# A table of experts with one entry a tile, and the loop of the expert stage written out

## The chip, the cores and the metric

One of the eight cores of a Trainium2 chip runs the kernel. The time is the core's device time in microseconds (us); smaller is better. The engines are TensorE (PE; PEld is its loading of weights), VectorE (DVE), ScalarE (ACT), GpSimd (POOL) and SyncE (SP). Each has its own queue of instructions, and semaphores tie them together. A letter q behind an engine (ACTq, PEldq, DVEq, POOLq, SPq) marks what its queue does itself: register arithmetic, waits on semaphores, branches, loads of registers, the issue of DMAs.

## What is computed

A block of cross-attention with a gate, and behind it a mixture of experts with a gate. 8192 tokens (128 sequences of 64) of width 128; 16 heads of 64; 14 experts with a hidden width of 256, one expert a token.

```python
x = x + tanh(g_xattn[0]) * attention(layernorm(x), ctx_768, ...)     # 16 heads, D = 128
# then, over the rows n of layernorm(x), and added to x with the gate tanh(g_ffn):
logits = h @ router_w                                  # (8192, 14)
assignments = argmax(logits, axis=-1)
weights = softmax(logits)[assignments]
hid = gelu(einsum('nd,edf->nef', h, w1) + b1)          # F = 256
out = einsum('nef,efd->ned', hid, w2) + b2
moe_out = out[n, assignments[n]] * weights[n]
```

Only the expert that a token chose is worked out. The rest of the document is about that part.

## The kernel before

**Attention and routing.** The attention runs over 32 groups of 256 tokens (64 pairs of 128), from 0 to about 664 us. As the groups are done, DVE finds each token's expert, and POOL scatters the token's rows (the normalised row, the row itself, the weight, the token's number) into `rows_dram`, where every expert has a region of its own. When the counts are known, the regions are cut into tiles of 128 rows, 77 of them at most (`TILES`), and a table says for every tile in which row it starts (`row_tab`) and which expert it has (`expert_tab`).

**The table.** DVE works out both columns, with one tile a partition. PE turns them into a row in PSUM (`table_T`, L1251 to L1256): the rows' column by a transpose, the experts' column by a matmul with `pack`, a 128 x 32 matrix of powers of 16, so that four experts stand in one word, four bits each. POOL builds `pack` (`pack_rows`, L608 to L614). DVE copies the two rows into SBUF (`table_1_out`, L1671, for the first 16 tiles; `table_2_out`, L1788, for the others). An engine that needs an expert's number loads words of the table into its registers (`entries`, L297; the load is L304), shifts the word and masks it (the function `expert` in `ffn_run`, and `unit_expert`), and works out an address in the weights with one more register instruction (FUSED_REGOPS or ISA in the rows).

**The first 16 tiles ("units").** They belong to tiles that are full early. Their steps are placed by hand between the last steps of the attention, from about 664 to 709 us: `unit_T` (PE, L1271), `unit_copy` (ACT, L858), `unit_w1` (SP copies the expert's w1 into one of four buffers), `unit_W1` (PE, L1282), `unit_gelu` (ACT, L870), `unit_W2` (PE, L1297), `unit_out` (DVE, L1804 and L1806), `send_out` (POOL, L620).

**The expert stage.** The other 61 tiles run from 709.3 to 826.3 us, in `ffn_run` (L309) on ACT, PE and DVE. In step t, PE transposes tile t (L1229), multiplies tile t-2 by w1 (L1236) and tile t-4 by w2 (L1245). ACT copies the transposed tile t (L845) and applies gelu to tile t-2 (L851). DVE copies the w1 of tile t's expert from `w1_sb` into one of four buffers (L1883, "the pick"), and adds bias, weight and residual for tile t-4 (L1889, L1891). POOL scatters the finished tile to its tokens with one indirect DMA (`send_out`, L616 to L621). SP loads the next rows (`load_rows`, L428) into one of 16 buffers, when the scatter of the tile that was in it has landed.

**What is a loop.** Tiles are taken in trips of 16 (`RING`). In `ffn_run` the first trip of the stage (tiles 16 to 31) is written out with constants in its waits; trips 2 and 3 are a hardware loop, in which the waits are compared with a register; the rest is written out again. On POOL trips 1 to 3 are a loop, on SP trips 2 and 3. In `ffn_run` each trip begins with a load from `expert_tab`: four words in the first, then five words that begin one word before a group of four. The names QT, KT, V, xf, zx in rows are buffers that the attention used before.

Of the kernel before, what the change touches and what calls it, by code (L numbers as in the profile page):

```python
# [33 lines left out]
P = 128  # L34
# [9 lines left out]
PACK = 4  # L44
# [3 lines left out]
def gated_block_kernel(nc, x, ctx768, g_xattn, g_ffn, g_x, b_x, g_c, b_c, Wq, Wk, Wv, Wo,  # L48
# [29 lines left out]
    with ExitStack() as stack:  # L78
# [76 lines left out]
        pack = sb("pack", [P, P // PACK])  # L155
# [5 lines left out]
        row_tab_1, expert_tab_1 = sb("row_tab_1", [1, UNITS], I32), sb("expert_tab_1", [1, UNITS // PACK], I32)  # L161
        expert_tab = sb("expert_tab", [1, P // PACK], I32)
# [72 lines left out]
        s_pack, s_link1, s_cols1, s_tab1T, s_tab1 = sem("s_pack"), sem("s_link1"), sem("s_cols1"), sem("s_tab1T"), sem("s_tab1")  # L235
# [11 lines left out]
        f_send = sem("f_send")  # L247
# [85 lines left out]
        def unit_expert(eng, words, j):  # L333
            return eng.snap((words[j // PACK] >> (4 * (j % PACK))) & (SLOTS - 1))
# [5 lines left out]
        def _(sp):  # L340
# [53 lines left out]
            def unit_w1(j):  # L394

                e = unit_expert(sp, words, j)
# [36 lines left out]
            def load_trip(v, count):  # L433
                for i in range(count):
                    if i % PACK == 0:
                        starts = entries(mybir.EngineType.SP, row_tab, (v - 1) * RING + i, PACK, E * REGION)
                    load_rows(starts[i % PACK], i, v)

            for i in range(RING):
                load_rows(first_starts[i], i, 1)  # L440
            with sp.Fori(2, TRIPS) as v:
                load_trip(v, RING)
            load_trip(TRIPS, TILES - TRIPS * RING)
# [3 lines left out]
        def _(pool):  # L447
# [160 lines left out]
            def pack_rows():  # L608

                pool.memset(pack[:, :], 0.0).then_inc(s_pack, 1)  # L610
                for n in range(PACK):
                    pool.wait_ge(s_pack, n + 1)
                    pool.affine_select(out=pack[:, :], in_=pack[:, :], compare_op=ALU.not_equal, fill=float(SLOTS ** n), base=-n,
# [35 lines left out]
            with pool.Fori(1, TRIPS) as v:  # L649
                for i in range(RING):  # L650
                    send_out(v * RING + i, i)
# [1268 lines left out]
```

## Time and profile before

| | us |
|---|---|
| median of 3 runs | 828.7 (828.1 to 828.8) |
| the profiled execution, its own time | 832.4 |
| its span, from first to last instruction | 830.7 |
| attention and routing | 0 to about 664 |
| the 16 units, beside the end of the attention | 664 to 709.3 |
| expert stage, 61 tiles | 709.3 to 826.3 (117.0) |
| last scatter and end | 826.3 to 830.7 |

How to read it: the profiled execution's own time is 1.7 us longer than its span and 3.7 us longer than the median; a change is worked out as a difference of the profiled execution and then put on the median. All times in the text are from the start of the span.

### The profile page before, as it was taken

The page shows a single profiled execution, that of the slowest core. Times are in us where ns is not written, and L with a number is a line of the kernel's source. Part 1 is how long each engine was busy: PE and PEld are TensorE (multiplying, and loading weights), DVE is VectorE, ACT ScalarE, POOL GpSimd, SP SyncE. Part 2 cuts the span into 40 slices and gives each one's busy share as a digit, 9 for nine tenths or more (in the row PEclk, how much of TensorE's full clock was granted, in tenths as well). Part 3 has the DMA queues.
Part 4 walks back from the last instruction along what each step waited for, and adds up shares of the span by engine and source line. Part 5 has one row for each costly group of instructions (what it writes and reads, how often), then busy time and mean ns, then how long its engine had stood idle before and what let it go on. Part 6 is the DMA issues. An engine that isn't in the chain of part 4 may idle for free.

```text
span 830.7 us, 34251 instructions
## 1 busy us (share of the span) xinstructions
PE 764.7 (92%) x12698; PEld 691.8 (83%) x12699; DVE 570.7 (69%) x1518; ACT 565.9 (68%) x1172; POOL 476.4 (57%) x1038
## 2 busy tenths in 40 slices
PE   6889999999999999999999999999999977768775
PEld 6678999998899989999898999998998866657765
DVE  5366777777777777777777777777778855444444
ACT  3677877777777777777777777777777553444442
POOL 2555566666666555565666566655666545355455
PEclk8999999999999999999999999999999998787887
DMA  4740011011110111111010000010000243433330
GB/s 122 242 125 21 20 34 32 30 33 34 36 31 30 30 35 36 31 36 30 30 30 30 30 30 30 30 30 30 21 22 28 87 153 109 120 98 96 107 87 21
DMA packets 52308, 45.82 MB, mean 55 GB/s; under 512 B 14726, under 2 KB 47783, under 8 KB 52250
## 3 DMA queue, kind: packets, MB, share of 16 engines
q1 hardware_dynamic: 45770, 32.23, 13.9%
q0 software_dynamic: 5536, 12.80, 4.4%
q8 instruction: 36, 0.59, 0.3%
q14 instruction: 22, 0.18, 0.1%
q10 hardware_dynamic: 944, 0.01, 0.1%
HBM read 28.15 MB, written 15.48 MB: 53 GB/s over the span
## 4 chain that ended last, share of the span: by engine, by line
PE 84%; issue 4%; ACT 2%; another core or an unknown queue 1%; DVE 1%; ACTq 0%; POOL 0%; DMA 0%; DVEq 0%; POOLq 0%
PE psJ L960 11%; PE psJ L961 10%; PE psJ L962 10%; PE psS L1019 9%; PE psO L1059 8%; PE psT L1084 8%; PE psO L1245 4%; PE psM L1093 3%; PE psM L1094 3%; PE psM L1101 3%; PE psM L1236 2%; PE psT L1236 2%; PE psM L1124 1%; PE psM L971 1%
## 5 line engine op out<-in xcount | busy, mean ns | idle before, releaser
L521 POOL TENSOR_TENSOR probs<-probs,row_inv 128x1024 f32<-128x1024 f32 x63 | 119.7, 1900 | 22.7 <-DVE row_inv L1487 14.2
L684 ACT ACTIVATE QT<-psJ 128x512 f32<-128x512 f32 x128 | 76.4, 598 | 54.0 <-PE psJ L962 47.6
L1495 DVE TENSOR_TENSOR OT_l<-psO,OT_h 128x1024 fp32r<-128x1024 f32 x60 | 73.5, 1225 | 51.3 <-ACT OT_h L723 51.3
L684 ACT ACTIVATE KT<-psJ 128x512 f32<-128x512 f32 x128 | 77.4, 604 | 40.9 <-PE psJ L962 40.2
L1482 DVE TENSOR_REDUCE row_sum<-probs 128x16 f32<-128x1024 f32 x63 | 76.8, 1219 | 38.6 <-ACT probs L736 38.6
L730 ACT ACTIVATE PTs<-psT 128x512 f32<-128x512 f32 x126 | 75.8, 602 | 29.6 <-PE psT L1084 29.6
L1446 DVE TENSOR_REDUCE row_max<-psS 128x16 f32<-128x1024 f32 x63 | 76.2, 1210 | 17.4 <-PE psS L1019 17.4
L1019 PE MATMUL psS<-KT,QT 64*64 64x64 f32 x4032 | 82.8, 224 | 4.4 <-issue 1.0
L1019 PEld LDWEIGHTS psS<-KT,QT 64*64 64x64 f32 x4032 | 70.4, 136 | 17.6 <-issue 13.7
L1084 PE MATMUL psT<-ident,probs 128*128 128x128 f32 x504 | 80.1, 281 | 2.2 <-ACT PTs L730 1.9
L736 ACT ACTIVATE probs<-probs 128x1024 f32<-128x1024 f32 x63 | 66.4, 1054 | 21.9 <-DVE probs L1453 21.9
L564 POOL DMA_INDIRECT rows_by_expert<-rows,place_i x64 | 64.5, 1007 | 24.9 <-issue 24.8
L960 PE MATMUL psJ<-CT_h,Wk_h 96*128 96x256 f32 x256 | 77.4, 302 | 1.5 <-ACT QT L684 1.4
L960 PE MATMUL psJ<-XT_h,Wq_h 128*128 128x256 f32 x256 | 77.9, 304 | 0.1
L684 ACT ACTIVATE V<-psJ 128x512 f32<-128x512 f32 x128 | 75.4, 611 | 3.6 <-PE psJ L962 3.4
L1453 DVE TENSOR_TENSOR probs<-psS,row_max 128x1024 f32<-128x1024 f32 x63 | 76.8, 1220 | 1.2
L1059 PE MATMUL psO<-PTs,V 64*64 64x64 f32 x4096 | 74.9, 220 | 1.6 <-issue 0.9
L1059 PEld LDWEIGHTS psO<-PTs,V 64*64 64x64 f32 x4096 | 66.9, 135 | 6.2 <-issue 2.1
L961 PE MATMUL psJ<-CT_l,Wk_h 96*128 96x256 f32 x256 | 71.8, 280 | 0.0
L961 PE MATMUL psJ<-XT_l,Wq_h 128*128 128x256 f32 x256 | 71.7, 280 | 0.0
L962 PE MATMUL psJ<-XT_h,Wq_l 128*128 128x256 f32 x256 | 71.5, 279 | 0.0
L962 PE MATMUL psJ<-CT_h,Wk_l 96*128 96x256 f32 x256 | 71.5, 279 | 0.0
(297 smaller groups left out, 2165.7 us busy)
## 6 DMA issues: line engine op xcount, KB each, us to landing
V<-rows_by_expert SPq DMA_DIRECT2D x42, 129.0 KB
QT<-rows_by_expert SPq DMA_DIRECT2D x35, 129.0 KB
x_in<-in_x_dram SPq DMA_DIRECT2D x32, 128.0 KB, 2.2
x_res<-in_x_dram SPq DMA_DIRECT2D x32, 128.0 KB, 2.1
c_in<-in_ctx_dram SPq DMA_DIRECT2D x32, 96.0 KB, 2.3
KT<-w_sb SPq DMA_DIRECT2D x16, 128.0 KB, 2.0
rows_by_expert<-pad_row SPq DMA_DIRECT2D x1, 1806.0 KB, 11.6
w_sb<-in_L_ffn_w_dram SPq DMA_DIRECT2D x1, 1792.0 KB, 8.7
```

The source lines that it names most:

```text
L521: pool.tensor_tensor(pr, pr, row_inv[:, p.k % 2, :].unsqueeze(2).to_broadcast([P, 16, SEQ]), ALU.mult).then_inc(s_norm, 1)
L684: act.activation(dst, psJ[n % 2][:, :], ACT.Copy).then_inc(s_jobev, 1)
L730: act.activation(PTs[:, (p.k - 1) % 2, half, :], bank[:, :], ACT.Copy).then_inc(s_ptev, 1)
L960: pe.matmul(outs, w_h, r_h, start=True, stop=False)
L961: pe.matmul(outs, w_h, r_l, start=False, stop=False)
L962: return pe.matmul(outs, w_l, r_h, start=False, stop=True)
L1019: last = pe.matmul(psS[64 * c:64 * c + 64, col:col + SEQ], QT[part, p.par(), 2 * g + c, tok], KT[part, p.par(), 2 * g + c, tok], start=Tru ...
L1059: last = pe.matmul(psO[64 * h:64 * h + 64, 512 * b + SEQ * m:512 * b + SEQ * m + SEQ], V[part, p.par(1), p.k % 2, head * DH:head * DH + DH ...
L1084: last = pe.transpose(bank[:, P * g:P * g + P], src, ident[:, :])
L1446: dve.tensor_reduce(row_max[:, :], bank[:, :].rearrange("p (n k) -> p n k", k=SEQ), AX.X, ALU.max).then_inc(s_max, 1)
L1453: dve.tensor_tensor(probs[:, p.k % 2, :, :], psS[:, :].rearrange("p (n k) -> p n k", k=SEQ), row_max[:, :].unsqueeze(2).to_broadcast([P, 1 ...
L1482: dve.tensor_reduce(row_sum[:, :], pr, AX.X, ALU.add).then_inc(s_sum, 1)
```

## The change

The table has one entry a tile, and is no longer packed: `expert_tab` grows from 32 to 128 words, `expert_tab_1` from 4 to 16. `table_T` makes two transposes in place of a transpose and a matmul; `pack`, `pack_rows` and the semaphore `s_pack` go. An engine loads the entries of 16 to 20 tiles at once and uses them as they are, with no shift and no mask. The loops of `ffn_run`, of SP and of POOL are written out, all waits of the stage are against constants, and SP loads 16 starts of rows a trip, not four at a time. In `send_out` the increment of `f_send`, on which nothing waited, goes.

```diff
-        def ffn_run(eng, engine, ffn):
-            def experts(words, i):
-                def expert(n):
-                    at = PACK + i - n
-                    return eng.snap((words[at // PACK] >> (4 * (at % PACK))) & (SLOTS - 1))
-                return expert
-            words = [None] + list(entries(engine, expert_tab, 0, RING // PACK, 2 ** 16 - 1))
+        def ffn_run(engine, ffn, behind, ahead):
+            def experts(values, i):
+                return lambda n: values[behind + i - n]
             for i in range(RING):
-                ffn(UNITS + i, 1, i, [i - n >= 0 for n in range(5)], experts(words, i))
-            with eng.Fori(2, TRIPS) as v:
-                words = entries(engine, expert_tab, (v - 1) * (RING // PACK) - 1, RING // PACK + 1, 2 ** 16 - 1)
-                for i in range(RING):
-                    ffn(v * RING + i, v, i, [True] * 5, experts(words, i))
-            words = entries(engine, expert_tab, (TRIPS - 1) * (RING // PACK) - 1, RING // PACK + 1, 2 ** 16 - 1)
-            for t in range(TRIPS * RING, TILES + 4):
-                ffn(t, t // RING, t % RING, [t - n < TILES for n in range(5)], experts(words, t - TRIPS * RING))
+                if i == 0:
+                    values = [None] * behind + list(entries(engine, expert_tab, 0, RING - ahead, SLOTS - 1))
+                ffn(UNITS + i, 1, i, [i - n >= 0 for n in range(5)], experts(values, i))
+            for t in range(2 * RING, TILES + 4):
+                if t % RING == 0:
+                    count = min(RING - ahead, TILES - t) + behind
+                    values = list(entries(engine, expert_tab, t - UNITS - behind, max(count, 1), SLOTS - 1))
+                ffn(t, t // RING, t % RING, [t - n < TILES for n in range(5)], experts(values, t % RING))
...
-            return list(entries(engine, expert_tab_1, 0, UNITS // PACK, 2 ** 16 - 1))
-        def unit_expert(eng, words, j):
-            return eng.snap((words[j // PACK] >> (4 * (j % PACK))) & (SLOTS - 1))
+            return list(entries(engine, expert_tab_1, 0, UNITS, SLOTS - 1))
...
-                e = unit_expert(act, words, j)
+                e = words[j]
...
-                pool.sem_inc(f_send, 1)
...
-            pack_rows()
...
-            with pool.Fori(1, TRIPS) as v:
-                for i in range(RING):
-                    send_out(v * RING + i, i)
-            for t in range(TRIPS * RING, TILES):
+            for t in range(UNITS, TILES):
                 send_out(t, t % RING)
...
-                pe.matmul(psM[0:1, P:P + P // PACK], cols[:, 1:2], pack[:, :], start=True, stop=True).then_inc(done, 1)
+                pe.transpose(psM[0:1, P:2 * P], cols[:, 1:2], ident[:, :]).then_inc(done, 1)
...
-                dve.tensor_copy(expert_tab[:, :], psM[0:1, P:P + P // PACK]).then_inc(s_tab, 1)
+                dve.tensor_copy(expert_tab[:, :], psM[0:1, P:2 * P]).then_inc(s_tab, 1)
...
-            ffn_run(act, mybir.EngineType.Activation, ffn)
+            ffn_run(mybir.EngineType.Activation, ffn, 2, 2)
...
-            ffn_run(pe, mybir.EngineType.PE, ffn)
+            ffn_run(mybir.EngineType.PE, ffn, 4, 4)
...
-            ffn_run(dve, mybir.EngineType.DVE, ffn)
+            ffn_run(mybir.EngineType.DVE, ffn, 4, 0)
```

In words: a trip loads 16 entries on ACT (14 in the stage's first trip, 15 in its last), 16 on PE (12 in the first), and on DVE 16 in the first trip, 20 in the next two and 17 in the last. PE and DVE begin their loads at a word whose number divides by four, ACT at word 14, 30 and 46. At t = 80 PE and DVE load one more word each.

On DVE, at the start of the expert stage. Before, the load is four words, and a word is taken apart ahead of each pick:

```order
L304 TENSOR_LOAD expert_tab [waits s_tab]
L1883 REGISTER_ALU [waits f_w1]
L1883 ISA
L1883 COPY KT<-w1_sb 128x256
L1883 REGISTER_ALU [waits f_w1]
L1883 REGISTER_ALU
L1883 ISA
L1883 COPY KT<-w1_sb 128x256
```

And now, where the load is 16 words:

```order
L302 TENSOR_LOAD expert_tab [waits s_tab]
L1853 ISA [waits f_w1]
L1853 COPY KT<-w1_sb 128x256
L1853 ISA [waits f_w1]
L1853 COPY KT<-w1_sb 128x256
L1853 ISA [waits f_w1]
L1853 COPY KT<-w1_sb 128x256
```

The one or two REGISTER_ALU instructions ahead of each ISA are gone, and the wait now stands on the ISA that works out the address.

On ACT, in the middle of the stage, the gelu of a tile (KT is the hidden layer). Before:

```order
L845 ACTIVATE xf<-psJ 128x128 [waits f_t1]
L851 REGISTER_ALU [waits f_w2,f_w1]
L851 REGISTER_ALU
L851 ISA
L851 ACTIVATE KT<-psT,b1_sb 128x128
L851 ISA
L851 ACTIVATE KT<-psT,b1_sb 128x128
```

And now:

```order
L816 ACTIVATE xf<-psJ 128x128 [waits f_t1]
L822 ISA [waits f_w2,f_w1]
L822 ACTIVATE KT<-psM,b1_sb 128x128
L822 ISA
L822 ACTIVATE KT<-psM,b1_sb 128x128
```

Two register instructions between the wait and the ACTIVATE are gone; the order of the other work is the same. The units' gelu (L870) changes in the same way.

On PE, at the turn of the loop. Before, the branch and the load of five words stand between two tiles:

```order
L1245 MATMUL psO<-w2_sb,KT 128x128
L321 REGISTER_ALU
L321 COMPARE_AND_BRANCH
L304 TENSOR_LOAD expert_tab
L1229 MATMUL psJ<-ident,QT 128x128 [waits f_load0,f_t1ev]
L1236 MATMUL psM<-zx,KT 128x128 [waits f_gelu,f_pick,f_t1ev]
```

And now:

```order
L1216 MATMUL psO<-w2_sb,KT 128x128
L302 TENSOR_LOAD expert_tab
L1200 MATMUL psJ<-ident,QT 128x128 [waits f_load0,f_t1ev]
L1207 MATMUL psM<-zx,KT 128x128 [waits f_gelu,f_pick,f_t1ev]
```

The branch is gone; the load is still there, and is longer.

## Rows read from the trace of the kernel before

**Rows 1.** The page's fourth part: the chain that ended last, by engine.

```profile
PE 84%; issue 4%; ACT 2%; another core or an unknown queue 1%; DVE 1%; ACTq 0%; POOL 0%; DMA 0%; DVEq 0%; POOLq 0%
```

**Rows 2.** Stretches: from:to, length, busy us (count) by engine, clock, DMA.

```profile
664.00:709.30 45.30, 33.19 (x300) 28.67 (x301) 24.23 (x117) 19.46 (x61) 21.35 (x27) 0.88 0.43 132
709.30:826.30 117.00, 85.72 (x550) 78.85 (x548) 55.29 (x185) 50.58 (x183) 60.03 (x61) 0.82 0.32 90
```

**Rows 3.** Chain of waits from 664 us: start, duration, what; the units.

```profile
690.10 0.04 ACTq L870
690.13 0.03 issue
...
693.34 0.04 ACTq L870
...
693.40 0.04 ACTq L870
...
701.96 0.04 DVEq L1804
```

**Rows 4.** The table's loads (L304), 650 to 700 us: shortest/median/longest ns.

```profile
L304 SPq TENSOR_LOAD <-row_tab x2: 989/1084/1179, 654.1 to 699.5; - x2
...
L304 PEldq TENSOR_LOAD <-expert_tab x1: 518/518/518, 664.4 to 664.4; - x1
```

**Rows 5.** The same, 700 to 716 us: the start of the expert stage.

```profile
L304 PEldq TENSOR_LOAD <-expert_tab x1: 351/351/351, 708.4 to 708.4; - x1
L304 DVEq TENSOR_LOAD <-expert_tab x1: 354/354/354, 710.2 to 710.2; - x1
```

**Rows 6.** The same, 730 to 737 us: the first loads of five words.

```profile
L304 PEldq TENSOR_LOAD <-expert_tab x1: 1362/1362/1362, 733.0 to 733.0; - x1
L304 ACTq TENSOR_LOAD <-expert_tab x1: 1128/1128/1128, 734.2 to 734.2; - x1
```

**Rows 7.** DVE in order of time, start of stage: start, busy, work [idle before].

```profile
710.76 1.18 DVE L1883 COPY KT<-w_sb 128x256 f32 x4 [0.24 <-issue]
```

**Rows 8.** PE in order of time: start of stage, and turn of the loop.

```profile
711.15 1.19 PE L1236 MATMUL psM<-xf,KT 128*128 128x128 f32 x4 [0.62 <-ACT zx L845]
...
765.66 0.47 PE L1229 MATMUL psJ<-ident,QT 128*128 128x128 f32 x1 [0.67 <-issue]
```

**Rows 9.** DVE in order of time: the row that ends each long wait.

```profile
723.44 0.29 DVE L1889 TENSOR_TENSOR ysum<-psO,b_sb 128x128 f32<-128x128 f32 x1 [3.97 <-remote]
...
731.00 0.29 DVE L1889 TENSOR_TENSOR ysum<-psO,b_sb 128x128 f32<-128x128 f32 x1 [4.03 <-remote]
...
738.71 0.29 DVE L1889 TENSOR_TENSOR ysum<-psO,b_sb 128x128 f32<-128x128 f32 x1 [1.55 <-PE psO L1245]
...
746.34 0.29 DVE L1889 TENSOR_TENSOR ysum<-psO,b_sb 128x128 f32<-128x128 f32 x1 [3.31 <-remote]
```

**Rows 10.** POOL in order of time: the scatters of four tiles.

```profile
724.99 1.01 POOL L620 DMA_INDIRECT out_dram<-QT  x1 [2.67 <-DVE QT L1891]
726.31 0.98 POOL L620 DMA_INDIRECT out_dram<-QT  x1 [0.30 <-issue]
...
728.88 0.98 POOL L620 DMA_INDIRECT out_dram<-QT,V  x1 [0.31 <-issue]
732.55 1.02 POOL L620 DMA_INDIRECT out_dram<-QT,V  x1 [2.69 <-DVE QT L1891]
```

**Rows 11.** One line: what POOL's queue does for L619.

```profile
L619 POOLq EVENT_SEMAPHORE  x77: 17/17/17, 672.1 to 826.6; - x77
```

**Rows 12.** Waits from 710 to 826 us: total, times, longest.

```profile
ACT KT L851 <- remote: 12.6, 4, 4.3
...
PE psO L1245 <- ACT KT L851: 9.5, 8, 2.3
```

**Rows 13.** One line: POOL building the packing matrix (L613).

```profile
L613 POOL TENSOR_SCALAR_AFFINE_SELECT pack<-pack x4: 212/212/213, 644.1 to 645.2; 128x32 f32<-128x32 f32 x4
```

More of the change, by code:

```diff
@@ L154, in gated_block_kernel @@
         row_tab = sb("row_tab", [1, P], I32)
-        pack = sb("pack", [P, P // PACK])
         ends_1, full, cum_1, move_1 = sb("ends_1", [P, E], I32), sb("full", [P, E]), sb("cum_1", [P, E]), sb("move_1", [P, E])
@@ L160, in gated_block_kernel @@
         expert_1, row_1, cols_1 = sb("expert_1", [P, 1]), sb("row_1", [P, 1]), sb("cols_1", [P, 2])
-        row_tab_1, expert_tab_1 = sb("row_tab_1", [1, UNITS], I32), sb("expert_tab_1", [1, UNITS // PACK], I32)
-        expert_tab = sb("expert_tab", [1, P // PACK], I32)
+        row_tab_1, expert_tab_1 = sb("row_tab_1", [1, UNITS], I32), sb("expert_tab_1", [1, UNITS], I32)
+        expert_tab = sb("expert_tab", [1, P], I32)
         b1_rows = sb("b1_rows", [E * FK, P])
@@ L234, in gated_block_kernel @@
         s_row_tab = sem("s_row_tab")
-        s_pack, s_link1, s_cols1, s_tab1T, s_tab1 = sem("s_pack"), sem("s_link1"), sem("s_cols1"), sem("s_tab1T"), sem("s_tab1")
+        s_link1, s_cols1, s_tab1T, s_tab1 = sem("s_link1"), sem("s_cols1"), sem("s_tab1T"), sem("s_tab1")
         s_soft = sem("s_soft")
@@ L246, in gated_block_kernel @@
         f_w2, f_sum, f_out = sem("f_w2"), sem("f_sum"), sem("f_out")
-        f_send = sem("f_send")
         NEWT = 5 + 4 * NEWTON + 1
@@ L394, in unit_w1 @@
             def unit_w1(j):
-                e = unit_expert(sp, words, j)
+                e = words[j]
                 if j >= 4:
@@ L431, in load_rows @@
                 sp.dma_start(tile_rows[i], rows_dram[bass.ds(r, P), :]).then_inc(f_load[i], 16)
[L433 to L437, printed above, removed]
-            for i in range(RING):
[L440 to L443, printed above, removed]
+            for t in range(UNITS, TILES):
+                if t % RING == 0 and t > UNITS:
+                    first_starts = entries(mybir.EngineType.SP, row_tab, t - UNITS, min(RING, TILES - t), E * REGION)
+                load_rows(first_starts[t % RING], t % RING, t // RING)
         @block.gpsimd
@@ L606, in _ @@
             run(pool, step)
[L608 to L613, printed above, removed]
-                                       pattern=[[-PACK, P // PACK]], channel_multiplier=1).then_inc(s_pack, 1)
             def send_out(t, i):
                 pool.wait_ge(f_out, t + 1)
-                pool.sem_inc(f_send, 1)
                 pool.indirect_dma_start(out_rows, bass.IndirectOffsetOnAxis(tile_rows[i][:, ROW - 1:ROW].bitcast(I32), 0),
@@ L648, in _ @@
             send_out(15, 15)
-            with pool.Fori(1, TRIPS) as v:
-                for i in range(RING):
-                    send_out(v * RING + i, i)
-            for t in range(TRIPS * RING, TILES):
+            for t in range(UNITS, TILES):
                 send_out(t, t % RING)
@@ L860, in unit_gelu @@
             def unit_gelu(j):
-                e = unit_expert(act, words, j)
+                e = words[j]
                 at = [act.snap(e * FK + k) for k in range(FK)]
@@ L1251, in table_T @@
             def table_T(cols, ready, count, done):
-                pe.wait_ge(s_pack, PACK + 1)
                 pe.wait_ge(ready, count)
                 pe.transpose(psM[0:1, 0:P], cols[:, 0:1], ident[:, :])
-                pe.matmul(psM[0:1, P:P + P // PACK], cols[:, 1:2], pack[:, :], start=True, stop=True).then_inc(done, 1)
+                pe.transpose(psM[0:1, P:2 * P], cols[:, 1:2], ident[:, :]).then_inc(done, 1)
             def b1_T():
@@ L1286, in unit_W2 @@
             def unit_W2(j):
-                e = unit_expert(pe, words, j)
+                e = words[j]
                 at = [pe.snap(e * F + k * D) for k in range(FK)]
@@ L1673, in table_1_out @@
                 dve.tensor_copy(row_tab_1[:, :], psM[0:1, 0:UNITS]).then_inc(s_tab1, 1)
-                dve.tensor_copy(expert_tab_1[:, :], psM[0:1, P:P + UNITS // PACK]).then_inc(s_tab1, 1)
+                dve.tensor_copy(expert_tab_1[:, :], psM[0:1, P:P + UNITS]).then_inc(s_tab1, 1)
             def taken_1():
@@ L1791, in table_2_out @@
                 dve.tensor_copy(row_tab[:, :], psM[0:1, 0:P]).then_inc(s_row_tab, 1)
-                dve.tensor_copy(expert_tab[:, :], psM[0:1, P:P + P // PACK]).then_inc(s_tab, 1)
+                dve.tensor_copy(expert_tab[:, :], psM[0:1, P:2 * P]).then_inc(s_tab, 1)
             def unit_out(j):
-                e = unit_expert(dve, words, j)
+                e = words[j]
                 b2_at = dve.snap(e * D)
```

## The prediction

> **What bounds the kernel now.** I read the page's chain of waits first. PE holds 84% of it [rows 1], nearly all in the attention, whose instructions the change leaves alone. What it does touch lies behind 664 us: the 16 units (45.3 us) and the expert stage (117.0 us) [rows 2]. In the stage every engine is idle for much of the time: PE is busy 85.7 of 117.0 us, POOL 60.0, DVE 55.3, ACT 50.6 [rows 2]. So no engine's load sets its pace; the order of time must show what does.
>
> On DVE it shows that the stage goes by groups of four tiles. Four tiles pass quickly, then DVE waits for up to 4 us. The rows that end these waits stand at 723.44, 731.00, 738.71 and 746.34 us [rows 9]: 7.56, 7.71 and 7.63 us apart, 7.63 on the mean, or 1.91 us a tile. 61 tiles make 61/4 x 7.63 = 116.4 us, which is the stage. POOL has the same period: a scatter at 724.99, the next of the four 1.32 us later, the fourth from 728.88 to 729.86, then a wait of 2.69 us, and the next group at 732.55, 7.56 us after the last [rows 10]. Between the end of POOL's fourth scatter (729.86) and DVE's next row (731.00) lie 1.14 us, and from there to POOL's next scatter 1.55 us. What holds the signals back until POOL's group is over, the profile does not say (it calls the releaser "remote"); that DVE goes on 1.1 us after it is what rows show. I take the cycle to be: POOL's four scatters 4.87 us, 1.14 us, DVE and the way to POOL 1.55 us.
>
> **Writing out the loops: 0 us.** The trace holds the test. Tiles 16 to 31 are already written out, with constants in their waits, and the loop's first turn comes at 733 to 735 us, where the five-word loads stand [rows 6]. The first two spacings lie before that or across it (7.56, 7.71), the third in the loop (7.63) [rows 9]. At most 0.07 us a group speaks for the form without a loop, and one of the two spacings is longer. The turn of the loop leaves PE idle for 0.67 us ahead of a transpose [rows 8]; twice that, 1.3 us, is the bound of a gain if nothing hides it. The group's wait hides it: a turn falls into the 7.71, which is 0.08 us over the mean. I take 0.
>
> **Register instructions in the units: -0.8 us.** Here the steps of a unit wait for each other, and the chain of waits goes through ACT's queue. Ahead of a gelu stand one or two pieces of 0.04 us of L870 with 0.03 us of issue behind each: one at 690.10, two at 693.34 and 693.40 [rows 3]. The whole chain from 664 to 709.3 us holds eight such pieces on ACT and three of L1804 on DVE (one at 701.96 [rows 3]). The instruction that works out the address stays, and takes over the wait. 8 x 0.066 + 3 x 0.08 = 0.77 us. Bounds: 0, if the long waits in between take it up, and -2.1, if both steps of all 16 units were in line (16 x 2 x 0.066). I take -0.8.
>
> **The units' loads: +0.3 us.** They grow from 4 to 16 words. SP does load 16 words: 989 and 1179 ns, both in the list before 700 us; PE's load of four words takes 518 ns at 664.4 [rows 4]. PE's would end 0.5 to 0.7 us later, and the unit's first W1 stands 0.5 us behind the old end (665.44 in the chain), waiting for ACT's copy. That leaves 0.2 to 0.4 us: +0.3. The bound below is 0 (the attention's matmuls behind it are ready and give it back), the one above is in the rival.
>
> **The start of the stage: +0.75 us.** The pick of tile 16 needs DVE's load. Now: four words, 354 ns from 710.2 us [rows 5], pick at 710.76 [rows 7], PE's first W1 at 711.15 [rows 8], 0.1 us after that pick ends (711.05). The load grows to 16 words; at SP's 989 to 1179 ns [rows 4] everything behind moves by 0.64 to 0.83 us. I take 0.75. PE's own load (351 ns at 708.4 [rows 5], now 12 words, so at most SP's 989) and ACT's (14 words) end before that, so their delays are inside it. The shift and the mask ahead of the pick go as well, 0.1 us at most, and are inside the rounding.
>
> **POOL's step in the cycle: -1.0 us.** `send_out` loses the increment of a semaphore, 17 ns [rows 11], which stands between DVE's signal and the scatter. A step in a queue costs its own time and the issue gap behind it, 0.03 to 0.05 us where the chain lists it [rows 3]. 0.07 us, once a group, is 15 x 0.07 = 1.0 us. Bounds: 0 (the wait only moves to the next instruction) and -1.2. In the four scatters themselves it gains nothing, since they follow at 1.29 to 1.32 us with the queue ahead of them.
>
> **The stage's other loads: 0.** At t = 32, 48 and 64 the engines load 15 to 20 words instead of five. The five words take 1128 to 1362 ns [rows 6], more than SP's 16 (989): their start, one word before a group of four, is what makes them dear, and PE's and DVE's new loads begin on such a group. 16 words would cost 0.1 to 0.4 us less than now, 20 about as much. ACT's still begin off a group of four. On all three, the present loads fall into the 7.71 us spacing and cost 0.08 us at most. I take 0; the bounds are -0.2 and, for ACT, the rival. The one-word loads of PE and DVE at t = 80 lie ahead of the last W2, for which PE waits for ACT, as it does before other W2s [rows 12].
>
> **The table: 0.** POOL no longer builds `pack`: four steps of 212 ns at 644 us [rows 13], ahead of a wait of POOL. The second transpose has 128 columns in place of 32, and DVE's two copies are longer by a tenth or two of a microsecond; PE's path gets 0 to +0.2 us. POOL's loss of 1 us of work at 644 us is no gain, since the chain runs through PE there [rows 1]. SP's 16 starts at once instead of 4 x 0.3 us delay one row load by 0.7 us, 14 tiles before it is needed.
>
> **The sum.** -0.8 + 0.3 + 0.75 - 1.0 = -0.75, so the profiled execution would take 832.4 - 0.75 = 831.7 us. That execution is 3.7 us above the median of the runs shown; put on the median, the forecast is 828.7 - 0.8 = **827.9 us**. A measurement of this kernel tells about 0.2% from no change, 1.7 us: below 827.0 is faster, above 830.4 slower.
>
> **Rivals.**
> - *The cycle does not shorten.* If the release comes by its own clock, POOL's step gives nothing: +0.3 + 0.75 - 0.8 = +0.25, 829.0 us. The wait that moves to the next instruction speaks for it; the 0.3 us gap between scatters that no work fills also does [rows 10].
> - *The whole hand-over gets shorter (faster).* If the cycle runs over ACT and PE as well, the shift and the mask ahead of gelu (0.13 us) and of W2 (0.15 to 0.19) come out of each group: 15 x 0.28 more, about -4 us, 824 us. For it: ACT waits "remote" up to 4.3 us, and W2 waits for gelu 8 times [rows 12]. Against it: DVE's long waits end in an ysum whose W2 had been done long before, and no register step of PE is between.
> - *A load is priced by the word (slower).* Five words that begin off a group of four cost 1128 to 1362 ns [rows 6], 0.23 to 0.27 a word. ACT's three loads of 15 or 16 words begin off a group too. By the word they take 4.0 us each, 2.9 more than now. ACT's cover is its wait in a group, up to 4.3 us but 3.1 on the mean (12.6/4) [rows 12], of which 1.1 are used; so 0.9 us each come through on the mean and 2.9 at worst: +2.7 to +8.6. It decides from a load of about 3 us. With the forecast's other terms: 830.6, and up to 836 us. If all loads went by the word, DVE's at the start would cost 4.0 instead of 0.35 us, +3.65, and PE's at 664.4 +3.2; SP's 16 words in 989 ns [rows 4] speak against that. The Trainium skill (Runtime: NRT & Kernel Launch, Instruction fetch mechanics) gives about 200 ns a register even for a bulk load. By that figure, as an estimate, 16 words take 3.2 us and the start of the stage alone would lose 2.8 us. SP's row [rows 4] does not agree with it, 62 to 74 ns a word, while the five words [rows 6] do.
> - *The wait of every fourth tile goes away.* If the loop or `f_send` were behind it, the stage would run at POOL's 1.29 to 1.32 us a tile [rows 10], 61 x 1.29 = 79 us, and save 38. Against it: the waits are there in the part without a loop, too, from 723 us on [rows 9].
> - *The change does nothing to the time*: the register steps hide behind longer waits everywhere, and the loads too: 828.7.
>
> **How the numbers follow.** Forecast 0.40 (827 to 829, of it 0.14 below 827.0). Cycle as it was 0.20, nothing at all 0.04. Shorter hand-over 0.15. Load by the word 0.18, of it 0.13 above 830.4 and 0.05 (a mild one) below it. The wait gone 0.03. Faster: 0.14 + 0.15 + 0.03 = 0.32. Slower: 0.13, and 0.07 from the cases near +0.3 us whose start of the stage costs more than I think, 0.20. The same: 0.48. The range reaches to the shorter hand-over (824.0) on one side and to the load by the word with 1.4 us behind 830.6 on the other, 832.0; outside lie the lost wait, a third of the loads' case and a little on either side of the second rival, 0.2 in all.
>
> **What would show it.** In the changed profile: the units' first tile 0.3 us later and the last one 0.5 us earlier; DVE's load at 710 us about 1.0 us long, and PE's first W1 0.75 us further behind it; ACT's loads at t = 32, 48, 64 at 1.0 to 1.3 us (4 us means the rival); no two-step gap ahead of L822; DVE's long waits still every fourth tile, 7.56 us apart in place of 7.63. If the spacing is 7.3 us or less, the hand-over was longer than I read; if it is 7.63, POOL's step was free. The forecast is wrong at its root if the groups of four change their size or go away, since then the cover on which each 0 above rests is gone.

## The result

The changed kernel takes 817.98 us (median of 4 runs, 815.99 to 821.41), the kernel before beside it 828.4 (825.89 to 828.8). The ratio is 0.9886, with a 95% interval of 0.9864 to 0.9909. Two later comparisons gave 0.9832 (0.9778 to 0.9887) and 0.9867 (0.9837 to 0.9896). The change makes the kernel 1.1 to 1.7% faster, 9 to 14 us, where the forecast was 0.8 us and the range ended at 824.

The profiled execution of the changed kernel has a time of 821.4 us and a span of 819.6. Two stretches, as in [rows 2] (from:to, length, busy us and count of PE, PEld, DVE, ACT, POOL, then clock, share of the DMA engines, GB/s):

```profile
665.60:709.10 43.50, 32.01 (x273) 27.84 (x272) 23.69 (x112) 19.38 (x61) 20.89 (x26) 0.88 0.49 147
709.10:814.70 105.60, 77.66 (x549) 70.22 (x549) 53.77 (x184) 49.23 (x183) 60.49 (x61) 0.92 0.33 94
```

The matmuls, copies and scatters are the same in both kernels, but TensorE's granted clock is not: it was 0.82 in the stage before [rows 2] and is 0.92 here, and with it PE's busy time fell by 8 us. Whether that is a cause of the gain or goes with it is taken up with the put-back kernels below. The units (from the first `unit_T` to the first transpose of the stage) take 43.5 us, where they took 44.6; the expert stage 105.6 us, where it took 117.0. The rest of the difference in span is 1.5 us less in the attention, which the change leaves alone, against 2.4 us more in the first hundred and 0.5 us more behind the stage; the first hundred differ from run to run (POOL's first scatter stands between 102.3 and 107.5 us in the traces of this study). So almost all of the gain is in the expert stage, and that is the length that the experiments are compared by.

DVE's rows that answer to [rows 9] (start, busy, work, idle before and its releaser):

```profile
723.03 0.29 DVE L1859 TENSOR_TENSOR ysum<-psO,b_sb 128x128 f32<-128x128 f32 x1 [3.43 <-remote]
...
728.97 0.29 DVE L1859 TENSOR_TENSOR ysum<-psO,b_sb 128x128 f32<-128x128 f32 x1 [1.98 <-PE psO L1216]
...
730.51 0.29 DVE L1859 TENSOR_TENSOR ysum<-psO,b_sb 128x128 f32<-128x128 f32 x1 [0.66 <-PE psO L1216]
...
732.03 0.29 DVE L1859 TENSOR_TENSOR ysum<-psO,b_sb 128x128 f32<-128x128 f32 x1 [0.49 <-remote]
...
733.55 0.29 DVE L1859 TENSOR_TENSOR ysum<-psO,b_sb 128x128 f32<-128x128 f32 x1 [0.47 <-PE psO L1216]
```

The first group of four is still there. The next does not come 7.6 us later, but after 5.9, and then tile follows tile at 1.52 to 1.54 us, with no long wait. POOL shows the same, against [rows 10]: a scatter follows the last by 1.29 us within a group, and by 1.5 us where the tiles come singly:

```profile
727.18 0.98 POOL L595 DMA_INDIRECT out_dram<-QT  x1 [0.31 <-issue]
728.47 0.98 POOL L595 DMA_INDIRECT out_dram<-QT,V  x1 [0.30 <-issue]
730.44 0.98 POOL L595 DMA_INDIRECT out_dram<-QT,V  x1 [0.99 <-issue]
731.98 0.98 POOL L595 DMA_INDIRECT out_dram<-QT,V  x1 [0.56 <-issue]
733.50 0.98 POOL L595 DMA_INDIRECT out_dram<-QT,V  x1 [0.54 <-issue]
```

Counted over the whole stage: pauses of more than 2.3 us from one scatter's start to the next split the 61 scatters into 15 runs in both traces of the kernel before, most often runs of four (11 and 7 of the 15), and into 8, 6 and 11 runs in the three traces of the changed kernel, with runs of up to 14, 31 and 9.

The table's loads, as in [rows 4 to 6] (shortest/median/longest in ns, first and last start):

```profile
L302 PEldq TENSOR_LOAD <-expert_tab x6: 308/1146/1290, 665.3 to 811.3; - x6
L302 DVEq TENSOR_LOAD <-expert_tab x6: 310/1360/1445, 669.6 to 813.9; - x6
L302 ACTq TENSOR_LOAD <-expert_tab x5: 1246/3387/3566, 654.7 to 785.7; - x5
```

16 to 20 words that begin on a group of four cost PE and DVE 1.1 to 1.4 us (the shortest, 0.31, are the one-word loads at t = 80). 15 or 16 words that begin off a group cost ACT 3.4 to 3.6 us, 0.22 to 0.23 a word. The third rival priced this load rightly, and it still did not make the kernel slower.

The hand-over to a gelu in the units, in the chain of waits, against [rows 3] (start, duration, what):

```profile
684.99 0.02 issue
685.01 0.05 ACTq L841
685.06 0.05 issue
685.11 0.06 ACT KT L841
```

One instruction is left between PE's signal and the ACTIVATE: 0.12 us, where two register instructions of 0.04 us and their gaps stood ahead of it.

### The profile page after: what moved, and what is told of

Same layout as the page of the kernel before. It is cut to its first block, busy times and chain, and to the rows that moved or that the text cites. A ratio compares the mean times of both kernels' runs of the same rounds, so it can differ in the third digit from the quotient of the medians.

```text
span 819.6 us, 33480 instructions
## 1 busy us (share of the span) xinstructions
PE 757.8 (92%) x12696; PEld 684.7 (84%) x12696; DVE 569.3 (69%) x1517; ACT 564.9 (69%) x1171; POOL 477.0 (58%) x1033
## 4 chain that ended last, share of the span: by engine, by line
PE 84%; issue 4%; ACT 2%; another core or an unknown queue 1%; DVE 1%; POOL 1%; DMA 0%; DVEq 0%; ACTq 0%; POOLq 0%
PE psJ L931 11%; PE psJ L932 10%; PE psJ L933 10%; PE psS L990 9%; PE psO L1030 8%; PE psT L1055 8%; PE psM L1064 3%; PE psM L1065 3%; PE psM L1072 3%; PE psO L1216 3%; PE psT L1207 2%; PE psM L1207 2%; PE psM L1095 1%; PE psM L942 1%
```

## The experiments

The length of the stage is that from the start of its first transpose on PE to the end of its last `ysum` (the sum of W2's product and the bias) on DVE. Three traces of the changed kernel have 105.6, 107.3 and 110.4 us, two of the kernel before 117.0 and 115.7. A single trace is thus good to some 2.5 us, and small differences are read from the ratios. A ratio's interval is not the whole of its uncertainty either: the changed kernel's own three ratios lie 0.5% (4.5 us) apart. The expectations name theories by letters: A, the shorter hand-overs are the gain; B, the written-out loops are; C, ACT's long loads break up the groups; D, POOL's step ahead of the scatter does.

### Which part of the change: the table alone

`ffn_run` loads 16 to 20 entries as in the changed kernel, within the loops of before; the loops of SP and POOL and the increment of `f_send` are as before.

```diff
-            for t in range(2 * RING, TILES + 4):
+            with eng.Fori(2, TRIPS) as v:
+                values = list(entries(engine, expert_tab, v * RING - UNITS - behind, RING - ahead + behind, SLOTS - 1))
+                for i in range(RING):
+                    ffn(v * RING + i, v, i, [True] * 5, experts(values, i))
+            for t in range(TRIPS * RING, TILES + 4):
```

> The register table alone (one entry a tile, no shift and mask), with all loops and POOL's semaphore increment as before. Theory A (the shorter hand-overs between ACT, PE and DVE break up the groups of four): most of the gain, 7 to 11 us below before, about 819 us. Theory B (the loops written out bring it): within 2 us of before, 827 to 830. Theory C (the long loads of ACT, 3.4 us in the changed kernel's trace, shift the engines against each other and break the groups): as A, since these loads are in this kernel too.

Measured: 0.9888 of before (0.9819 to 0.9957); stage 110.7 us.

### The loops alone

The packed table with its shifts and masks; every loop of the stage written out.

```diff
-            with eng.Fori(2, TRIPS) as v:
-                words = entries(engine, expert_tab, (v - 1) * (RING // PACK) - 1, RING // PACK + 1, 2 ** 16 - 1)
-                for i in range(RING):
-                    ffn(v * RING + i, v, i, [True] * 5, experts(words, i))
+            for t in range(2 * RING, TRIPS * RING):
+                if t % RING == 0:
+                    words = entries(engine, expert_tab, (t // RING - 1) * (RING // PACK) - 1, RING // PACK + 1, 2 ** 16 - 1)
+                ffn(t, t // RING, t % RING, [True] * 5, experts(words, t % RING))
...
-            with sp.Fori(2, TRIPS) as v:
+            for v in range(2, TRIPS):
...
-            with pool.Fori(1, TRIPS) as v:
-                for i in range(RING):
-                    send_out(v * RING + i, i)
-            for t in range(TRIPS * RING, TILES):
+            for t in range(UNITS, TILES):
```

> The packed table with its shifts and masks, all loops on ACT, PE, DVE, SP and POOL written out with constant waits. Theory A and C: no gain, 827 to 830 us, with a spacing of 7.6 us between groups of four. Theory B: 818 to 820 us.

Measured: 0.9967 (0.9941 to 0.9993); stage 113.4 us.

### POOL's part alone

The kernel before, with POOL's loop written out and `f_send` gone.

```diff
-                pool.sem_inc(f_send, 1)
...
-            with pool.Fori(1, TRIPS) as v:
+            for t in range(UNITS, TILES):
```

> The kernel before with POOL's part of the change alone: its loop written out, and the semaphore increment ahead of each scatter gone. Theory A and C: 0 to 1.2 us below before (the term of the prediction). Theory D (POOL's step ahead of the scatter decides whether its scatters stay in groups): 4 to 10 us below before.

Measured: 0.9969 (0.9941 to 0.9996); stage 113.9 us. The windows of the three, in the order of the text:

```profile
704.20:814.90 110.70, 81.42 (x550) 73.32 (x549) 53.51 (x186) 49.12 (x183) 59.48 (x60) 0.89 0.34 98
```

```profile
705.20:818.60 113.40, 80.68 (x549) 73.74 (x549) 53.20 (x184) 50.30 (x183) 60.51 (x61) 0.89 0.33 93
```

```profile
705.00:818.90 113.90, 80.82 (x550) 73.51 (x549) 56.16 (x186) 50.59 (x183) 60.02 (x61) 0.90 0.33 94
```

The table brings about 1.1% (0.4 to 1.8) of the 1.1 to 1.7; POOL's part and the loops 0.3% each, and since the loops' kernel contains POOL's loop written out, these two may be the same 0.3%. Theory B falls. Theory D asked for 4 to 10 us; POOL's part as a whole brought 2.6 (0.3 to 4.9). What the increment of `f_send` is worth by itself isn't shown: the loops' kernel still has it and gains as much as the kernel without it.

### The register instructions, put back one engine at a time

The changed kernel, with two masks that change no value ahead of the address in the expert stage, on ACT (gelu), PE (W2) and DVE (pick) or on one of them. The trace shows them where the shift and the mask stood, with the wait on the first: 122 register instructions on each engine, where the kernel before had 106 at each of these places (every fourth tile needs a mask alone). The 21 that it had ahead of DVE's `ysum` are not put back.

```diff
+        def ops(eng, e):
+            return eng.snap(((e & 31) & 15))
...
-                    e = expert(2)
+                    e = ops(act, expert(2))
...
-                    e = expert(4)
+                    e = ops(pe, expert(4))
...
-                    at = dve.snap(expert(0) * F)
+                    at = dve.snap(ops(dve, expert(0)) * F)
```

> The changed kernel with two register instructions put back (two masks that change nothing) ahead of every gelu's address on ACT, every W2's on PE and every pick's on DVE in the expert stage. Theory A (the register instructions in the hand-overs are what the table saves): the stage goes back to 111 to 115 us, the time to 0.993 to 1.0 of before. Theory F (they don't matter in the stage; what helps is where and how long the loads are, and the rest is chance): stage 105 to 109, time 0.983 to 0.990.

> The same, on ACT alone. If the path of a tile runs over the gelu (A): half or more of what all three bring, 0.988 to 0.995. If DVE's or PE's matter: as the changed kernel, 0.983 to 0.988.

> The same, on PE alone, ahead of W2. A: 0.987 to 0.993, less than or like ACT's. If PE's queue stands idle there anyway: as the changed kernel, 0.983 to 0.988.

> The changed kernel with the two register instructions put back on DVE alone, ahead of the pick. If the path of a tile runs PE, ACT, PE, DVE and not over the pick: as the changed kernel, 0.983 to 0.988, stage 105 to 108 us. If the pick is on the path: 0.988 to 0.993, stage 109 to 113.

> The two register instructions ahead of the pick on DVE alone, a second time. If the pick is on the path of a tile: 0.3 to 0.6% above after_third. If not: within 0.2% of it.

Measured: all three 0.9975 (0.9958 to 0.9992); ACT alone 0.9924 (0.9901 to 0.9946); PE alone 0.9899 (0.9879 to 0.9919); DVE alone 0.9915 (0.9887 to 0.9943) and, a second time, 0.9887 (0.9852 to 0.9921). The stages of all, ACT and PE:

```profile
709.30:824.70 115.40, 80.70 (x549) 73.59 (x549) 52.92 (x184) 50.11 (x183) 62.46 (x62) 0.87 0.31 87
```

```profile
709.60:821.90 112.30, 82.41 (x549) 74.97 (x549) 52.72 (x184) 50.59 (x183) 60.10 (x60) 0.87 0.31 89
```

```profile
706.10:817.00 110.90, 80.17 (x550) 71.63 (x549) 54.28 (x184) 49.38 (x183) 60.86 (x61) 0.90 0.32 90
```

With all three, the stage is as long as that of before (115.7 and 117.0), and nearly the whole gain is gone, though the table, its loads and the written-out loops are those of the changed kernel. Its waits from 709 to 824.7 us are nearly those of before again (total, times, longest):

```profile
POOL out_dram L599 <- DVE QT L1865: 35.8, 17, 5.5
DVE ysum L1863 <- remote: 29.4, 10, 4.0
```

The same two in the kernel before, from 710 to 826 us:

```profile
POOL out_dram L620 <- DVE QT L1891: 40.5, 18, 5.1
DVE ysum L1889 <- remote: 28.5, 8, 4.0
```

And in the changed kernel, from 709 to 815 us:

```profile
POOL out_dram L595 <- DVE QT L1861: 24.0, 12, 5.4
DVE ysum L1859 <- remote: 15.9, 8, 4.9
```

With all three put back, the scatters stand in 15 runs again, 9 of them of four.

So theory A stands: what the table saves is the two register instructions in the hand-overs. Against 0.9862, the mean of the three comparisons of the changed kernel, ACT's are worth 0.6% (5 us, or 0.08 us a tile), PE's 0.4%, DVE's 0.2 to 0.5%, all three 1.1%. The sum of all three is clear: its interval (0.9958 to 0.9992) lies above those of all three comparisons of the changed kernel. How it divides among the engines is less so, since the changed kernel did not run beside ACT's and PE's kernels: against its highest ratio, 0.9886, ACT's are worth 0.4% and PE's 0.1%. That all three cost more than each alone (0.9975 against 0.9924, 0.9899 and 0.9915) says that they don't wholly hide each other. DVE's is the least certain: side by side with the changed kernel (0.9867 there) its second run is 0.2% above it, with intervals that overlap, and its traces have stages of 108.1 and 107.9 us, in the middle of the changed kernel's.

The rival is PE's clock, which was 0.82 and 0.84 in the two traces of before and 0.92, 0.89 and 0.86 in those of the changed kernel. It does not order the stages. With all three put back the clock is 0.87 and PE is busy for 80.7 us, and the stage takes 115.4; the third trace of the changed kernel has 0.86 and 82.7 us of busy PE, and its stage takes 110.4. The loops' and POOL's kernels have 0.89 and 0.90, and stages of 113.4 and 113.9. So the clock by itself doesn't explain the difference; whether it adds to it is not shown.

### ACT's long loads

The changed kernel, with ACT's loads begun on a group of four.

```diff
-            ffn_run(mybir.EngineType.Activation, ffn, 2, 2)
+            ffn_run(mybir.EngineType.Activation, ffn, 4, 2)
```

> The changed kernel, with ACT's table loads starting at a multiple of four words (12, 28, 44) and 18 entries long. Each load should fall from 3.4 us to 1.0 to 1.4 us. Theory A: as fast as the changed kernel or up to 6 us faster (three loads, 2 us each), 812 to 818. Theory C: the gain is lost, 825 to 830.

Measured: 0.9856 (0.9813 to 0.9898), stage 109.2 us.

```profile
L302 ACTq TENSOR_LOAD <-expert_tab x5: 1232/1364/1485, 649.3 to 781.2; - x5
```

The start of the load off a group of four is what made it dear: 18 words on a group take less than half of 16 off it. Theory C falls, since the gain stays. And the 2 us saved three times don't show in the time either. In the changed kernel ACT's idle time ahead of the copy after such a load is 3.05 us:

```profile
732.71 0.63 ACT L822 ACTIVATE KT<-psT,b_sb 128x128 f32<-128x128 f32 x2 [0.54 <-PE psT L1207]
736.38 0.28 ACT L816 ACTIVATE xf<-psJ 128x128 f32<-128x128 f32 x1 [3.05 <-issue]
```

POOL meanwhile works off the tiles that DVE had finished; that for this reason less or nothing of the wait reaches the end is my reading, and no run shows it.

### What holds PE's signals

In the first stretch of the stage, PE and ACT of the changed kernel:

```profile
719.28 0.27 PE L1200 MATMUL psJ<-ident,V 128*128 128x128 f32 x1
719.39 0.61 PE L1207 MATMUL psT<-zx,KT 128*128 128x128 f32 x4
719.84 0.61 PE L1216 MATMUL psO<-w_sb,KT 128*128 x4
```

```profile
720.80 0.63 ACT L822 ACTIVATE KT<-psM,b_sb 128x128 f32<-128x128 f32 x2 [1.30 <-issue]
722.89 0.28 ACT L816 ACTIVATE xf<-psJ 128x128 f32<-128x128 f32 x1 [1.47 <-remote]
```

By its record the transpose ended at 719.55 us, and ACT was free from 721.43, but its copy began at 722.89, 3.3 us after the transpose. DVE's ysum at 723.03, for a product whose record ends before 719.5, came at the same time. POOL was at four indirect DMAs from 717.11 to 722.06 us, the last two of them begun after the transpose had ended. Three kernels ask which part of the scatter does it. In their expectations theory P says that POOL's work on an indirect DMA holds PE's signals, theory L that the transfers do. The first replaces the indirect scatter by a plain DMA from POOL's queue to fixed rows:

```diff
-                pool.indirect_dma_start(out_rows, bass.IndirectOffsetOnAxis(tile_rows[i][:, ROW - 1:ROW].bitcast(I32), 0),
-                                        tile_out[i], None, bounds_check=TOK - 1, oob_is_err=False).then_inc(f_scat[i], 16)
+                pool.dma_start(out_rows[P * (t % 64):P * (t % 64) + P, :], tile_out[i]).then_inc(f_scat[i], 16)
```

> The changed kernel, with POOL's indirect scatter of a finished tile replaced by a plain DMA from POOL's queue to fixed rows of the output (so the tokens' order is left out; the bytes and all waits stay). Theory P (PE's completion signals are held while POOL works on an indirect DMA): the waits of 2.3 us and more on DVE go away, PE's pace of 1.0 us a tile sets the stage, and it falls from 106 us to 62 to 80. Theory L (the transfers themselves, the row loads of SP above all, hold them): the stage stays at 100 us or more.

Measured: 0.9426 (0.9376 to 0.9475); the stage takes 74.4 us.

```profile
699.40:773.80 74.40, 66.43 (x549) 63.70 (x549) 51.59 (x184) 48.44 (x183) 32.50 (x61) 0.98 0.52 150
```

```profile
727.79 0.29 DVE L1858 TENSOR_TENSOR ysum<-psO,b_sb 128x128 f32<-128x128 f32 x1
...
728.79 0.29 DVE L1858 TENSOR_TENSOR ysum<-psO,b_sb 128x128 f32<-128x128 f32 x1
...
729.79 0.29 DVE L1858 TENSOR_TENSOR ysum<-psO,b_sb 128x128 f32<-128x128 f32 x1
```

A tile a microsecond, PE's own pace, and the groups are gone; no wait of DVE for W2 is over 2.3 us. More than one thing changes here: POOL is busy for 0.54 us a scatter in place of 0.98, the rows go to other places, and PE's clock is 0.98 in place of 0.92, with 11 us less of busy time on PE. The second kernel keeps the indirect scatter and takes nearly all bytes out of SP's row loads:

```diff
-                sp.dma_start(tile_rows[i], rows_dram[bass.ds(r, P), :]).then_inc(f_load[i], 16)
+                sp.dma_start(tile_rows[i][:, ROW - 2:ROW], rows_dram[bass.ds(r, P), ROW - 2:ROW]).then_inc(f_load[i], 16)
```

> The changed kernel, where SP's row loads of tiles 32 to 76 bring only the last two of 258 columns (with the token's number; the rest of the rows stays that of an older tile, so most of the rows' data is left out). The number of transfers, waits and scatters stays, the bytes loaded fall to under 1%. Theory P: the stage stays near 106 us, with the long waits. Theory L: the stage falls below 90 us.

Measured: 0.9849 (0.9794 to 0.9905), stage 102.9 us, with 35 GB/s in place of some 95:

```profile
703.00:805.90 102.90, 79.36 (x549) 71.72 (x549) 54.76 (x186) 49.24 (x183) 59.94 (x61) 0.90 0.15 35
```

The loads' bytes are worth little or nothing; theory L falls as far as the loads go. The third kernel scatters only the first 64 rows of each of the 61 tiles:

```diff
+                n = P if t < UNITS else P // 2
-                pool.indirect_dma_start(out_rows, bass.IndirectOffsetOnAxis(tile_rows[i][:, ROW - 1:ROW].bitcast(I32), 0),
-                                        tile_out[i], None, bounds_check=TOK - 1, oob_is_err=False).then_inc(f_scat[i], 16)
+                pool.indirect_dma_start(out_rows, bass.IndirectOffsetOnAxis(tile_rows[i][0:n, ROW - 1:ROW].bitcast(I32), 0),
+                                        tile_out[i][0:n, :], None, bounds_check=TOK - 1, oob_is_err=False).then_inc(f_scat[i], 16)
```

> The changed kernel, with only the first 64 rows of each of the 61 tiles scattered (half of their output is left out). If the hold lasts as long as POOL works on an indirect DMA, and that follows the number of rows: each takes 0.5 to 0.6 us in place of 0.98, and the stage falls to 75 to 92 us. If POOL's time stays at 0.98 us and the stage at 104 to 108, the rows moved don't matter; if POOL's time halves and the stage stays, the hold isn't POOL's time.

Measured: 0.9893 (0.9866 to 0.992), stage 111.4 us. The time of an indirect DMA on POOL hardly falls with the rows, 906 ns for 64 against 983 for 128:

```profile
L596 POOL DMA_INDIRECT out_dram<-QT,V x42: 900/906/1029, 688.8 to 816.1; - x42
```

So half of the rows bring nothing, and this run could not tell POOL's time and the rows apart as it was meant to: none of my three cases came as written, since POOL's time hardly fell with the rows halved. What is shown: with plain DMAs in place of the indirect ones the stage is 31 us shorter than in the changed kernel's first trace, and neither the bytes loaded nor the number of rows scattered accounts for it. That POOL's work on an indirect DMA is what holds PE's signals fits all three runs but is not shown, and by which path it would do so stays open.

### Scatters kept apart

A memset of a tile that nobody reads behind each scatter, so that POOL's scatters can't follow at 1.29 us; then the same with ACT's loads on a group of four.

```diff
+                if t >= UNITS:
+                    pool.wait_ge(s_pace, t - UNITS)
+                    pool.memset(pace[:, :], 0.0).then_inc(s_pace, 1)
```

> The changed kernel, with a memset of 128x256 on a tile that nobody reads behind each scatter of the expert stage, on POOL, some 0.3 us each. In the changed kernel's trace the stage runs at 1.5 us a tile wherever scatters stand 1.5 us apart, and falls into groups wherever they follow at 1.29. Theory P with a window: with scatters kept apart PE's signals get through between them, few waits over 2.3 us are left, and the stage takes 93 to 100 us, 5 to 12 less than now. If only the sum of POOL's busy time counts: 61 x 0.3 = 18 us longer at most, 106 to 124 us.

> The changed kernel with the memset behind each scatter (the paced run) and ACT's loads on a group of four words. In the paced run's trace POOL goes at 1.51 us a tile, 61 x 1.51 = 92 us, and the stage takes 103.7, with 11 us lost about the three loads of ACT (3.4 us each). If these loads cost what they look like: 3 x 2 = 6 us less than paced, stage 96 to 99 us, 0.974 to 0.978 of before. If PE's and DVE's loads (1.1 to 1.4 us) cost as much: no more than 2 us less.

> The memset of 0.34 us behind each scatter, a second time. If keeping the scatters apart helps: 0.2 to 0.6% below after_third, stage 102 to 105 us. If it only trades the hold for POOL's time: within 0.2% of it.

Measured: 0.9824 (0.9784 to 0.9864) and, the second time, 0.9842 (0.9812 to 0.9872); with the aligned loads 0.9854 (0.9828 to 0.988). The stages are 103.7, 102.8 and 105.4 us.

```profile
703.60:807.30 103.70, 78.78 (x549) 70.67 (x549) 56.21 (x186) 49.72 (x183) 80.59 (x119) 0.91 0.36 103
```

I had expected 93 to 100 us if the scatters' spacing matters and 106 to 124 if only POOL's busy time counts; the first run fell between the two. POOL works 20 us more and the stage of the two paced kernels is 2 to 8 us shorter than the changed kernel's three, which speaks for the theory that PE's signals get through between scatters. Only 2 and 3 of DVE's waits ahead of a `ysum` are over 2.3 us, where the changed kernel has 5, 7 and 8. In the time it is not clear: beside the paced kernels the changed one had 0.9832 and 0.9867, so the difference is 0.1 and 0.25%, and the intervals overlap. The aligned loads bring nothing here either; I had expected 6 us, having read ACT's idle time of 3 us as the cause of the pauses in the paced run.

The changed kernel itself, twice more:

> The changed kernel once more, beside the others on the same chip: a second trace of it. 0.983 to 0.991 of before; stage 103 to 110 us.

> The changed kernel beside the next two on one chip: 0.982 to 0.990 of before, stage 105 to 108 us.

Their stages are 107.3 us, as expected, and 110.4, longer than the 105 to 108 expected. And the kernel before, whose second trace has a stage of 115.7 us:

> The kernel before, a second trace. The four other traces with shift and mask (or their like) in the stage have stages of 113.4, 113.9 and 115.4 us; so 113 to 117 us here, with most waits of DVE in groups of four.

## Why the prediction was wrong

**What bounds the kernel: right in the place, wrong in the path.** The gain is in the units and the stage, and no engine's load sets the pace. But the cycle that I took for the stage (POOL's four scatters, 1.14 us, DVE and the way to POOL, together 7.56 us) is only a part of it. While POOL is at its group, PE, ACT and PE again still pass single tiles on to each other; how far they get, as I now read it, decides when the next group starts and how large it is. I had seen that ACT, too, waits for a remote signal [rows 12], and took the group's last wait for the only one that counts.

**The step that failed** is the sentence in the second rival's "against": that DVE's long waits end in a ysum whose W2 had been done long before, and no register step of PE stands between. That is true of the one wait at a group's start. It is not true of the other three tiles, where each gelu and each W2 begins with a register instruction behind the signal. The sum therefore has no term for the stage's 61 gelus, W2s and picks. Measured, it is 9 us (all three put back, 0.9862 to 0.9975), of which ACT's are about 5 us and PE's about 3 (3 and 1 against the changed kernel's highest ratio).

**The second rival** had the mechanism, but at 15 groups. By tiles, its own prices give 61 x 0.13 us for ACT = 8 us and 61 x 0.15 to 0.19 = 9 to 12 for PE; measured are about 5 and 3. By these estimates some six tenths of ACT's steps and three tenths of PE's count. Its gain of 4 us and its chance of 0.15 were both too small.

**The groups of four.** I named their going away as what would sink the forecast, and that is what happened: in the changed trace runs of tiles at 1.5 us stand among the groups. My bound for a stage without groups came from POOL's 1.29 us a tile, and so I gave it as a jump of 38 us with a chance of 0.03. The case between, some groups broken up, I didn't have. Nor did the prediction say anything of PE's clock, which moved from 0.82 to between 0.86 and 0.92.

**Writing out the loops: 0.** Measured 0.3% (0.1 to 0.6), 2.7 us, of which POOL's loop may be all. Nearly right; the first trip in the trace was a fair test for ACT, PE and DVE, but POOL's loop already holds tiles 16 to 63, so it was none for POOL. One thing stays open here: in the loops, too, register instructions stand at the waits (with those of the turns 86 on PE and 42 on ACT in the stage of before, none in the loops' kernel), and without them the gain was 0.3% with POOL's part. So not every register instruction at a wait counts like those ahead of gelu and W2.

**POOL's step: -1.0 us.** Measured -2.6 (-0.3 to -4.9), but with the register instruction of its loop gone too, and the loops' kernel, which keeps the increment, gained the same 0.3%. So the term is not confirmed: no run shows the increment's own worth.

**Register instructions in the units: -0.8; the units' loads: +0.3.** The units take 43.5, 41.7 and 41.9 us in the three traces of the changed kernel, 44.6 and 43.1 before: -1.5 on the mean. But the units run from 40.2 to 43.9 us in the other traces with the same units and scatters, and take 42.8 and 42.7 in the loops' and POOL's kernels, which have the old ones. The net of -0.5 has the right sign; its size can't be told from these traces.

**The start of the stage: +0.75.** Size of the load right, place wrong: DVE's load is 1.12 us long, but DVE is through with unit 15 earlier, by 0.5 us against the first transpose. The rows that answer to [rows 7] and [rows 8]:

```profile
710.85 1.16 DVE L1853 COPY KT<-w_sb 128x256 f32 x4 [0.93 <-issue]
```

```profile
711.24 1.20 PE L1207 MATMUL psM<-xf,KT 128*128 128x128 f32 x4 [0.82 <-ACT zx L816]
```

From the first transpose to the first W1 are 2.11 us, 0.23 more than the 1.88 before.

**The load by the word.** Right in its price for ACT's three loads (3.4 to 3.6 us; forecast 4.0), which was the mechanism with a chance of 0.18, wrong in what comes through: with the loads begun on a group of four, 2 us go from each, and the time does not move beyond its interval. The trace does not agree with the Trainium skill (Runtime: NRT & Kernel Launch, Instruction fetch mechanics) on a bulk load that begins on a group of four words: 1.1 to 1.4 us for 16 to 20 words is 0.07 a word. It is near its 200 ns a register for those that begin off a group (220 to 230).

## What to carry to other kernels

Where engines pass small pieces to each other and all of them are idle part of the time, count every instruction between a signal and the work that it releases, on each engine and for each tile, not once a cycle; two register instructions of 40 ns each (0.13 us with their gaps) were worth about 5 us of 828 on one engine alone. A repeating pattern in a trace (here four tiles and a wait) need not be a fixed cycle, and shorter hand-overs broke this one up. Before it is used as cover for a cost or as proof that something gives nothing, ask what one tile inside it waits for. And begin the loads of an unpacked table on a multiple of four words: 17 or 18 words then took 1.3 to 1.5 us where 15 or 16 took 3.4 to 3.6, though here the kernel's time did not show it.

## What the runs showed of the hardware

An indirect DMA on POOL takes 0.98 us for 128 rows and 0.91 for 64, so the number of rows hardly counts; with plain DMAs in its place the stage went from 105.6 us to 74.4. While POOL was at four of them in a row, PE's signals came 3.3 us (to ACT) and 3.6 us (to DVE) after the records of its matmuls ended; that one causes the other is not shown. One register instruction takes 0.04 us on ACT and, with the gap behind it, 0.06 to 0.07 from start to start. A load of registers costs 1.0 to 1.5 us for 16 to 20 words from a multiple of four, and 3.4 to 3.6 us for 15 or 16 words from elsewhere.
